# Fetched row sets by 28 products of 476 columns, and one place in PSUM for them

## What is computed

```python
h_fwd = h @ W_forward.T
h_rev = h @ W_reverse.T
src, dst = (adj[0], adj[1])
messages = h_fwd[src] * direction[:, 0:1] + h_rev[src] * direction[:, 1:2]
scores = jnp.einsum('ef,hf->eh', messages, attn_forward[0])
scores = jax.nn.leaky_relu(scores, negative_slope=0.2)
exp_scores = jnp.exp(scores - scores.max(axis=0, keepdims=True))
sum_exp = jax.ops.segment_sum(exp_scores, dst, num_segments=N)
norm = exp_scores / (sum_exp[dst] + 1e-10)
outs = [jax.ops.segment_sum(messages * norm[:, hd:hd + 1], dst, num_segments=N) for hd in range(H)]
```

## Time and profile before

| | us |
|---|---|
| median of 3 runs | 2936.72 (2936.69 to 2939.57) |
| the profiled execution | 2938.83 |
| its span | 2937.0 |
| TensorE busy | 2194.4 |
| VectorE busy | 1797.7 |
| GpSimd busy | 1630.8 |
| ScalarE busy | 432.5 |

### The profile page before, as it was taken

One profiled execution on the slowest core, in us unless ns is written; L12 is line 12 of the kernel. 1 busy time (PEld: TensorE's weight loads), 2 busy tenths in 40 slices (PEclk: granted clock), 3 DMA queues, 4 the chain that ended last, 5 costly groups with the idle time before them and its releaser, 6 DMA issues.

```text
span 2937.0 us, 48035 instructions
## 1 busy us (share of the span) xinstructions
PE 2194.4 (75%) x13105; PEld 1993.9 (68%) x13106; DVE 1797.7 (61%) x4481; ACT 432.5 (15%) x1222; POOL 1630.8 (56%) x1750
## 2 busy tenths in 40 slices
PE   6577877778787777787777777777873547999990
PEld 6476767767677676677677677676763446888880
DVE  6666665666565566566556566665654566666666
ACT  4000000000000000000000000000001432434344
POOL 6565565565665555656655656655653555333326
PEclk8789898898898898888888888988985558999995
DMA  5222222222222222222222222222223456556557
GB/s 184 52 53 49 51 51 50 51 52 50 50 53 50 49 51 50 51 48 53 52 48 51 52 50 52 52 50 49 54 48 121 137 174 186 200 187 206 192 170 264
DMA packets 176306, 256.67 MB, mean 87 GB/s; under 512 B 47079, under 2 KB 121000, under 8 KB 176005
## 3 DMA queue, kind: packets, MB, share of 16 engines
q0 software_dynamic: 53696, 121.60, 16.6%
q1 hardware_dynamic: 122564, 134.56, 14.9%
HBM read 218.11 MB, written 38.79 MB: 87 GB/s over the span
## 4 chain that ended last, share of the span: by engine, by line
DVE 29%; issue 26%; PE 24%; another core or an unknown queue 11%; DVEq 7%; DMA 2%; POOL 1%; ACT 1%; SPq 0%; ACTq 0%; POOLq 0%
PE p_hot L979 18%; DVE onehot L1070 5%; DVE shared L1000 3%; DVEq L1726 3%; DVE hot_ex L1042 2%; PE p_win L876 2%; DVE p_part L1008 2%; DVE rows L1081 1%; DVE rows L1005 1%; PE p_y L1894 1%; DVEq L867 1%; DVE p_y L1949 1%; PE p_h L1884 1%; DVE hot L1019 1%
## 5 line engine op out<-in xcount | busy, mean ns | idle before, releaser
L259 POOL DMA_INDIRECT rows<-node_table,index x1375 | 1303.7, 948 | 874.8 <-issue 470.6
L979 PE MATMUL p_hot<-parts,onehot 128*128 128x408 f32 (+1 forms) x6392 | 1410.1, 379 | 364.6 <-issue 192.8
L979 PEld LDWEIGHTS p_hot<-parts,onehot 128*128 128x128 f32 x6392 | 1288.8, 213 | 473.1 <-issue 263.2
L1070 DVE TENSOR_TENSOR onehot<-key,p_dve 128x1152 fp32r<-128x1152 f32 x376 | 473.8, 1281 | 108.8 <-PE p_hot L979 62.0
L1000 DVE TENSOR_TENSOR shared<-shared,p_win 65x64 f32 x784 | 170.9, 218 | 489.1 <-remote 382.0
L876 PE MATMUL p_win<-hot_ex,msg 128*65 128x64 f32 x3136 | 231.5, 228 | 165.1 <-issue 124.6
L876 PEld LDWEIGHTS p_win<-hot_ex,msg 128*65 128x65 f32 x3136 | 207.0, 142 | 196.8 <-issue 195.3
L940 ACT ACTIVATE rows<-p_hot,third 128x136 f32<-128x136 f32 x188 | 70.5, 375 | 1603.9 <-PE p_hot L979 990.5
L1081 DVE SCALAR_TENSOR_TENSOR rows<-p_hot,third,rows 128x136 f32<-128x136 f32 x376 | 134.9, 359 | 243.5 <-issue 192.3
L1735 POOL DMA_INDIRECT expert_rows<-ys,back x104 | 103.1, 992 | 269.4 <-DVE ys L1954 198.4
L1884 PEld LDWEIGHTS p_h<-xt,shared 128*128 128x128 f32 x1664 | 199.9, 194 | 33.9 <-ACT xt L1826 28.6
(11 more groups left out here) (270 smaller groups left out, 1419.0 us busy)
## 6 DMA issues: line engine op xcount, KB each, us to landing
shared<-in_w SPq DMA_DIRECT2D x120, 512.0 KB
rows<-node_table,index POOLq DMA_INDIRECT x1375
xs<-dispatched SPq DMA_DIRECT2D x104, 129.5 KB
key<-hot_keys SPq DMA_DIRECT2D x94, 128.0 KB
shared<-expert_rows SPq DMA_DIRECT2D x12, 896.0 KB, 7.8
token_rows<-in_x SPq DMA_DIRECT2D x7, 896.0 KB
shared<-in_x SPq DMA_DIRECT2D x7, 768.0 KB
out<-shared SPq DMA_DIRECT2D x6, 896.0 KB, 7.3
```

The lines of the kernel that those rows point to most:

```text
L259: pool.indirect_dma_start(out=rows[:, s, k, :], out_offset=None, in_=table, in_offset=bass.IndirectOffsetOnAxis(ap=index[:, s, 0, k:k + 1] ...
L979: last = pe.matmul(p_hot[:, j, 0:width * ROW], onehot[:, gr, :], parts[:, gr:NT:GP, m, :], start=(gr == 0 and m == 0), stop=(gr == ORDER[- ...
L1070: dve.tensor_tensor(onehot[:, a:b, :], key[:, s, j, :].unsqueeze(1).broadcast_to([P, b - a, P]), group_p[:, a:b].unsqueeze(2).broadcast_to ...
```

## The change

The 49 tiles are taken as 7 groups of 7 tiles. A product takes seven tiles of one direction d (68 columns each), so it has 476 columns and gives seven candidates; a set needs 7 groups, two parts and two directions, 28 products. `p_hot` is now one place of two banks, one for each direction, and `fetch` waits until the set before was kept (`hot_kept`). The one-hot has 7 blocks of 128 instead of 17, is made by one operation and has a buffer for each of the two sets. `keep` is VectorE's alone: a comparison of the candidates' numbers `place_no` with the edge's number `place`, multiplied in place into the candidates, for each direction; then, after its own signal, one reduction that adds the seven candidates into the row. ScalarE has no part in it. GpSimd works out keys and places once at the start with some more operations, and the engines that wait for them count to 18 instead of 12. The scratch for windows beyond the eighth, `p_x`, moves from `p_hot` to `p_dve`.

```diff
-GP = -(-NT // 3)
-HALF = -(-GP // 2)
-ORDER = list(range(HALF)) + list(range(NT - 2 * GP, GP)) + list(range(HALF, NT - 2 * GP))
+PLACES = 7
+GP = NT // PLACES
+assert GP * PLACES == NT
+assert 4 < PLACES <= 8
+KEYED = 18
...
-        third = esb("third", [P, 3, NF])
+        place = esb("place_of_source", [P, NF])
+        place_no = esb("place_no", [P, PLACES])
         key = esb("key", [P, RING, FILL, P])
-        onehot = esb("onehot", [P, GP, P], F32R)
+        onehot = esb("onehot", [P, FILL, GP, P], F32R)
...
-                pool.tensor_copy(third[:, 0, :], third[:, 0, :].bitcast(I32)).then_inc(s_init, 1)
-                pool.wait_ge(s_init, 4)
-                for m in range(2):
-                    pool.tensor_scalar(late[m], source, float((m + 1) * GP * P), float(GP * P), ALU.is_ge, ALU.mult)\
-                        .then_inc(s_init, 1)
-                for m in range(2):
-                    pool.tensor_scalar(third[:, m + 1, :], third[:, 0, :], float((m + 1) * GP * P), None, ALU.is_ge)\
-                        .then_inc(s_init, 1)
-                pool.wait_ge(s_init, 8)
-                pool.tensor_tensor(source, source, late[0], ALU.subtract).then_inc(s_init, 1)
-                pool.tensor_scalar(third[:, 0, :], third[:, 1, :], -1.0, 1.0, ALU.mult, ALU.add).then_inc(s_init, 1)
-                pool.wait_ge(s_init, 10)
-                pool.tensor_tensor(source, source, late[1], ALU.subtract).then_inc(s_init, 1)
-                pool.tensor_tensor(third[:, 1, :], third[:, 1, :], third[:, 2, :], ALU.subtract).then_inc(s_init, 1)
+                pool.tensor_copy(rest, place[:, :].bitcast(I32)).then_inc(s_init, 1)
+                n = 4
+                pool.wait_ge(s_init, n)
+                pool.tensor_copy(place[:, :], rest).then_inc(s_init, 1)
+                for much in (4, 2, 1):
+                    for of, by in ((source, late), (rest, step)):
+                        pool.tensor_scalar(by, of, float(much * GP * P), float(much * GP * P), ALU.is_ge, ALU.mult)\
+                            .then_inc(s_init, 1)
+                    n += 2 + (much == 4)
+                    pool.wait_ge(s_init, n)
+                    for of, by in ((source, late), (rest, step)):
+                        pool.tensor_tensor(of, of, by, ALU.subtract).then_inc(s_init, 1)
+                    n += 2
+                    pool.wait_ge(s_init, n)
+                pool.tensor_tensor(place[:, :], place[:, :], rest, ALU.subtract).then_inc(s_init, 1)
+                assert n + 1 == KEYED
...
-            p_hot = ps("p_hot", [P, FILL, 512])
-            p_x = p_hot[:, 0, TRIPLE * ROW:TRIPLE * ROW + HEADS * W]
+            p_hot = ps("p_hot", [P, 2, 512])
...
+            p_x = p_dve[:, 512 - HEADS * W:512]
...
-                        sp.wait_ge(hot_built, 2 * FILL * (c - 1))
+                        sp.wait_ge(hot_built, FILL * (c - 1))
...
-                    if coming(s, it, 1, 0):
-                        keep_first(c + 1, *coming(s, it, 1, 0))
                     act.wait_ge(score_ready, c + 1)
                     after(act, val_ready, c)
                     act.activation(ex_p, score[:, :, :], ACT.Exp, bias=neg_shift[:, 0:1])\
                        .then_inc(exp_ready, 1)
-                    if coming(s, it, 1, 1):
-                        keep_first(c + 1, *coming(s, it, 1, 1))
-
-                def keep_first(c, f, s, it, j):
-
-                    act.wait_ge(hot_rows, f + 1)
-                    after(act, msg_ready, c - RING + 1)
-                    act.activation(rows[:, s, KG + j, :], p_hot[:, j, 0:ROW], ACT.Copy, scale=third[:, 0, ds(f, 1)])\
-                       .then_inc(hot_third, 1)
...
-                    after(pe, hot_kept, 2 * (f - FILL + 1))
-                    for gr in ORDER:
-                        if gr in (0, ORDER[HALF]):
-                            pe.wait_ge(hot_built, 2 * (HOT + f) + 1 + (gr > 0))
-                        width = len(range(gr, NT, GP))
+                    after(pe, hot_kept, 2 * f)
+                    pe.wait_ge(hot_built, HOT + f + 1)
+                    for gr in range(GP):
                         for m in range(2):
-                            last = pe.matmul(p_hot[:, j, 0:width * ROW], onehot[:, gr, :],
-                                             parts[:, gr:NT:GP, m, :], start=(gr == 0 and m == 0),
-                                             stop=(gr == ORDER[-1] and m == 1))
-                        if gr == HALF - 1:
-                            last.then_inc(hot_half, 1)
+                            for d in range(2):
+                                last = pe.matmul(p_hot[:, d, 0:PLACES * COLS], onehot[:, j, gr, :],
+                                                 parts[:, gr:NT:GP, m, d * COLS:(d + 1) * COLS],
+                                                 start=(gr == 0 and m == 0), stop=(gr == GP - 1 and m == 1))
...
-                        second_half(*coming(s, it, 1, 1))
+                    if coming(s, it, 1, 0):
+                        keep(*coming(s, it, 1, 0))
...
-                        keep_others(*coming(s, it, 1, 0))
...
-                        keep_others(*coming(s, it, 1, 1))
+                        keep(*coming(s, it, 1, 1))
                     if coming(s, it, 2, 0):
-                        first_half(*coming(s, it, 2, 0))
-                        second_half(*coming(s, it, 2, 0))
+                        build_hot(*coming(s, it, 2, 0))
                     finish(c)
                     if coming(s, it, 2, 1):
-                        first_half(*coming(s, it, 2, 1))
-
-                def first_half(f, s, it, j):
+                        build_hot(*coming(s, it, 2, 1))
+
+                def build_hot(f, s, it, j):
 
                     dve.wait_ge(key_ready[s], 16 * it)
-                    after(dve, hot_half, f)
-                    build_hot(s, j, 0, HALF)
-
-                def second_half(f, s, it, j):
-
-                    after(dve, hot_rows, f)
-                    build_hot(s, j, HALF, GP)
-
-                def build_hot(s, j, a, b):
-
-                    dve.tensor_tensor(onehot[:, a:b, :],
-                                      key[:, s, j, :].unsqueeze(1).broadcast_to([P, b - a, P]),
-                                      group_p[:, a:b].unsqueeze(2).broadcast_to([P, b - a, P]), ALU.is_equal)\
+                    after(dve, hot_rows, f - FILL + 1)
+                    dve.tensor_tensor(onehot[:, j, :, :],
+                                      key[:, s, j, :].unsqueeze(1).broadcast_to([P, GP, P]),
+                                      group_p.unsqueeze(2).broadcast_to([P, GP, P]), ALU.is_equal)\
                        .then_inc(hot_built, 1)
 
-                def keep_others(f, s, it, j):
-
-                    dve.wait_ge(hot_third, f + 1)
-                    row = rows[:, s, KG + j, :]
-                    for m in range(1, 3):
-                        after(dve, hot_kept, 2 * f + m - 1)
-                        dve.scalar_tensor_tensor(out=row, in0=p_hot[:, j, m * ROW:(m + 1) * ROW],
-                                                 scalar=third[:, m, ds(f, 1)], in1=row, op0=ALU.mult, op1=ALU.add)\
-                           .then_inc(hot_kept, 1)
+                def keep(f, s, it, j):
+
+                    dve.wait_ge(hot_rows, f + 1)
+                    found = p_hot[:, :, 0:PLACES * COLS].rearrange("p d (v c) -> p d v c", v=PLACES)
+                    for d in range(2):
+                        last = dve.scalar_tensor_tensor(
+                            out=found[:, d], in0=place_no[:, :].unsqueeze(2).broadcast_to([P, PLACES, COLS]),
+                            scalar=place[:, ds(f, 1)], in1=found[:, d], op0=ALU.is_equal, op1=ALU.mult)
+                    last.then_inc(hot_kept, 1)
+                    dve.wait_ge(hot_kept, 2 * f + 1)
+                    dve.tensor_reduce(rows[:, s, KG + j, :].rearrange("p (d c) -> p d c", d=2),
+                                      found.rearrange("p d v c -> p d c v"), AX.X, ALU.add).then_inc(hot_kept, 1)
```

27 lines of the change are left out of this document (13 added, 14 removed).

## The result

| | before | after |
|---|---|---|
| median, us | 2938.14 (4 runs, 2936.69 to 2944.64) | 2985.22 (4 runs, 2979.1 to 2990.25) |
| ratio | | 1.0148 (95% interval 1.0126 to 1.0169) |
| span of the profiled execution, us | 2937.0 | 2977.3 |
| its edge loop, second to last start of the window sums | 135.4 to 2254.0 | 133.3 to 2294.0 |

In the profiled executions all of it lies in the edge loop: 2118.6 us became 2160.7, 42.1 us over 96 chunks, 0.44 each; ahead of it 2 us were gained and behind it 0.4 lost.

What follows compares the result with a forecast made beforehand. It took a ring of waits, not a full engine or memory, to bound the kernel. 25.5 us a chunk against 22.15, over 94 chunks, gave +315 us; with 3 at the start, about 3255 us, range 2960 to 3530.

Steps and rivals of the forecast that it cites:

- the first rival: Edge loop: TensorE's signals come promptly for the fetches, so a chunk takes 22.5 us, 2972 us in all; chance 0.2.
- The bound: Edge loop before: no engine or memory is full; a ring of waits with the gathers sets the pace, 22.15 us a chunk.
- Products: TensorE's fetch: six matmul starts fewer, taken as no gain, at most 0.77 us a fetch.
- One-hot: VectorE's build: two halves become one operation of 1.08 us, saving 1.5 us a set.
- Keep: VectorE's keep K: two operations of 0.71 us and a reduction of 1.55, 3.0 us together, between 2.6 and 3.7.
- Start: GpSimd's preparation: eight more operations, at most 7.5 us once, taken as 3 us.
- Order: Edge loop: TensorE's next fetch waits for VectorE's last keep, and late signals now meet VectorE's queue twice a chunk.
- The sum: One chunk of the loop added up: 25.4 us by the gathers, 26.8 with both signals late; 25.5 taken.
- one late in each chunk, the other now and then: The two fetches' signals to VectorE: the assumed lateness behind the 25.5 us taken for a chunk.
- Dear keep or a lower clock: Keep of 3.7 us, or TensorE's clock at 0.8: 27 to 29 us a chunk, 3390 to 3580; chance 0.17.
- About the same: All of TensorE's signals prompt, the window sum's too, no gather in the ring: 22.1 us a chunk, 2935; chance 0.05.
- two rings: Edge loop: one through score, gathers and window sums, 25.4 us; one through fetches and keeps, 26.8 with both signals late.

Runs made afterwards that it cites:

- e16: The kernel before with set 13 of each looped chunk not gathered, one gather less of fourteen: 2822.4 us, ratio 0.9597.
- e12: The changed kernel run again, unaltered, on another chip: 3017.6 us, ratio 1.0086 to the kernel before on that chip.
- e1: The changed kernel with the first set's keep moved behind the score on VectorE: 3010.6 us, ratio 1.0251.
- e2: The changed kernel without one of the two multiplying operations in the first set's keep: 2952.1 us, ratio 1.0047.
- e4: The changed kernel with eight gathers behind the window sums and six behind the score, instead of six and eight: 3049.0 us, ratio 1.0376.
- e7: The changed kernel with the second set's one-hot built ahead of the window sums instead of behind them: 3008.4 us, ratio 1.0056.
- e5: The changed kernel with sets 7 to 13 of each looped chunk not gathered, seven gathers less: 2962.2 us, ratio 0.9908.
- e6: The kernel before with sets 7 to 13 of each looped chunk not gathered, seven gathers less: 2405.5 us, ratio 0.8039.
- e3: The changed kernel without one of the two multiplying operations in the second set's keep: 2988.1 us, ratio 1.0169.
- e15: The changed kernel with set 13 of each looped chunk not gathered, one gather less of fourteen: 2851.5 us, ratio 0.9707.

## Why the prediction was wrong, point by point

**Right in sign, by a mechanism that it named, and wrong in size by a factor of seven.** The range, 2960 to 3530, holds 2985 near its lower end; the forecast of 3255 does not come near it. What came was the first rival, "signals prompt for the fetches", 22.5 us a chunk and 2972, with a chance of 0.2.

*The bound.* That the loop before is a ring of waits with the gathers in it is shown: e16 gives 1.25 us a chunk on the mean for one gather less, and the sums start 1.9 us behind the last gather in the kernel after as well.

*Products.* A fetch takes 6.3 to 9.2 us (median 6.36 for the first set and 7.92 for the second), 1402 us in all for 1410 before. No gain from six starts fewer, as taken.

*One-hot.* 1.08 us was forecast, 1077 ns measured.

*Keep.* 713 ns for each operation of 476, as forecast. The reduction takes 1149 ns where I took 1550: 1.21 ns for each of the 952 elements, as the contiguous row of PSUM had it (1092 ns for 896). K is 2.43 us (1021.49 to the next operation at 1023.92), not 3.0, and it stands in the sum twice. The strided row of SBUF was the wrong neighbour; the Trainium skill's cachelines (PSUM — Partial Sum Buffer, Specifications (TRN2)), whose sentence is on matmuls, did not carry over to a reduction on VectorE: the trace shows no charge for the step of 68 elements. That VectorE "comes out even" doesn't follow from the figures given with it, which add 1.6 us a chunk; the pages have 66.5 us more in all, 0.7 a chunk.

*Start.* Taken as 3 us lost; the loop began 2 us earlier (133.3 for 135.4). The pages count seven more operations of GpSimd (1757 for 1750), not eight.

*Order.* That TensorE would wait for the keep is right: 307.4 us that weren't there. The Trainium skill (TensorE: Matmul & The Clock Gate, A second HAM failure mode: psum-queue depth-cycling) speaks of throughput lost to the clock between matmul groups; here the granted clock in the loop is 0.87 for 0.88, so it cost about nothing on the mean, though a fetch of 7.93 us after an idle time of 3.03 (granted clock 0.78) and one of 6.36 after 1.83 (granted 1.00) stand side by side in one chunk.

*The sum.* The step that failed is "one late in each chunk, the other now and then": 3.0 us for the second fetch's signal or 1.6 for the first's, in each chunk of the changed kernel. In the kernel before that holds: of 62 chunks between 400 and 2000 us with a record of both signals, the first is over 0.5 us late in 25 and the second in 34, never both. It did not carry over. Measured, the first signal is at most 0.4 us late in the changed kernel, and the keep begins at most 0.15 us behind the second fetch in every chunk but nine, where that signal is about 6 us late. So the ordinary chunk is the first rival's sum with the keep at its measured 2.4: 0.8 + 0.8 + 11.7 + 6.2 + 2.4 = 21.9; the chunk of the timeline above has 6.04 to the end of the products, 2.43 keep, 0.80 score, 0.79 first gather, 11.54 to the next sums, 21.60. (The 2.5 for the products is right, though the subtraction beside it gives 2.3.) It is also the prediction's own sign of being wrong, a ring of 22.5 or below with the rows already signalled. That the rival's 2972 lies so near 2985 is partly luck: its keep is 0.6 us too dear, and the nine pairs of long chunks, which it doesn't have, cost 0.7 us a chunk.

What I had read as a property of TensorE's signals while gathers run depends on where in a run of gathers they fall, and on the pauses. In the kernel before, of 261 signals of fetches with a record between 400 and 2000 us (two a fetch), with runs less than 1.3 us apart counted as one, the 100 that fall up to two gathers into a run are 0.01 us late on the mean, and the 118 that fall six to nine gathers into one are 1.6 to 3.2; its runs at times almost touch (1.19 us between two at 1011.71). In the changed kernel the score and the second fetch start together behind the keep, so the fetch ends six or seven gathers into a run of eight, with a pause of 2.2 to 2.6 us on either side: 76 of 83 signals are at most 0.4 us late, and the seven others, 11 or 12 gathers into a run, 6.2 us on the mean. The count alone isn't the rule (six or seven gathers in, the one kernel is late and the other not). For the second fetch the pause ahead of the score's gathers decides, by the chunks of one and the same kernel: over the changed kernel, e12, e1, e2, e4 and e7, 150 to 2230 us, the signal is 3.0 to 7.5 us late in all 60 chunks without a pause (0.30 us) and at most 0.24 in the 170 with 2.1 us or more. But a pause is no general rule either: the first fetch's signal in e4 (1.4 us late on the mean), e5 (1.0) and e6 (2.7) is late five or six gathers into a run, with about 2 us or more of pause ahead of that run.

*The rivals.* "Dear keep or a lower clock" was not what came. "About the same", which needed the window sum's signal to come loose from the gathers, didn't come either: it is held in both kernels.

**Open.** Why a signal of TensorE waits for GpSimd's gathers no trace here shows, nor what lets the first fetch's signal through in one kernel and not in another. Nor why GpSimd starts some 3 us late; it does so at every 112th gather in the two kernels, at fourteen gathers a chunk, and in e5 and e6 at seven, so it goes by the gathers issued there, not by chunks or time. How the ordinary chunk's 22.0 us divides between the two rings isn't settled: e2, e3 and e7 fit two rings that are nearly tied, and show no more.

## What to carry to other kernels

A delay read off one schedule belongs to that schedule: before carrying it into a sum for another order, ask what it depended on (here, where in a run of gathers it fell and what pause stood ahead of that run) and look at the whole loop, chunk by chunk, not at two chunks. Where two rings of waits are nearly tied, a change of either is worth little, and a rare bad chunk can outweigh the mean of the others: a histogram of the loop's period shows it where busy times and means don't. It also shows whether the chunk of a timeline is the common one: the one first read of e4 was not.

## What the runs showed of the hardware that was not expected

- While GpSimd issues indirect gathers without a pause, TensorE's signals and late in the run its matmuls themselves can wait: window products stalled 0.4 to 1.2 us apiece in runs of fourteen, and the signals came 1.9 to 2.7 us behind the last gather. With half of the gathers gone, no keep began more than 1.4 us behind its fetch in the changed kernel, but the first signal was 2.7 us late on the mean in the kernel before.
- At every 112th gather, some 182 us apart in the changed kernel (246, 428, 611 us and so on), GpSimd starts some 3 us late with no wait that the profile shows; with thirteen gathers a chunk (e15) about 1 us at every 104th is all that is left of it.
- A reduction on VectorE with steps of 272 bytes in PSUM costs what a contiguous one does, 1.21 ns an element.
